# Spare rows for each skipped round of the expert tiles, integer row numbers by VectorE, and the last addition of x on Pool

## What is computed

```python
probs = softmax(flat @ gate_W)                    # flat: 2048 rows, 8 experts
topk_w, topk_idx = top_k(probs, 2); combine = one_hot(topk_idx) weighted, summed to 1
out = 0.5 * gelu(flat @ shared_W + shared_b)
for e in range(8):
    h = gelu(flat @ W1[e] + b1[e])
    out = out + combine[:, e:e + 1] * (h @ W2[e] + b2[e])
out = (out - mean) * rsqrt(var + eps) * gamma + beta
x = x + out
```

## Time and profile before

| What | us |
|---|---|
| Median of three timed runs | 948.01 |
| Lowest, highest | 945.2, 948.39 |
| The profiled execution: its own time | 945.59 |
| Its span, first to last instruction | 943.8 |

### The profile page before, as it was taken

The page is one execution under the profiler, slowest core; times in us unless marked ns, Lnnn a source line. Parts: engine busy times, 40 slices in busy tenths (PEclk is TensorE's granted clock), DMA queues, the critical chain, the costliest instruction groups (busy, mean ns, idle before and its releaser), DMA issues.

```text
span 943.8 us, 13190 instructions
## 1 busy us (share of the span) xinstructions
PE 797.0 (84%) x4073; PEld 392.5 (42%) x4074; DVE 389.8 (41%) x1042; ACT 413.8 (44%) x517; POOL 168.6 (18%) x161
## 2 busy tenths in 40 slices
PE   2876899999999999896979974289999999999820
PEld 1333223233222222232434443157666766666510
DVE  4793410111143343463445544264444444444227
ACT  2345488887898988633323321211111111111103
POOL 2030100100000000101004404772222222222330
PEclk9988799999999999987989987599999999999975
DMA  5759929874315320070021136454444444444334
GB/s 126 177 160 198 276 42 267 152 215 54 48 22 68 43 25 0 0 279 0 1 91 46 46 123 234 152 192 114 118 115 113 112 112 113 111 114 117 64 81 119
DMA packets 77288, 104.79 MB, mean 111 GB/s; under 512 B 9164, under 2 KB 62374, under 8 KB 77092
## 3 DMA queue, kind: packets, MB, share of 16 engines
q1 hardware_dynamic: 69948, 92.75, 38.4%
q0 software_dynamic: 7296, 11.47, 6.3%
HBM read 66.04 MB, written 38.16 MB: 110 GB/s over the span
## 4 chain that ended last, share of the span: by engine, by line
PE 66%; DVE 12%; DMA 7%; ACT 6%; issue 5%; SPq 2%; POOL 1%; ACTq 0%; POOLq 0%; DVEq 0%
PE ps L1833 12%; PE ps L1850 12%; PE ps L1548 9%; PE ps L1526 9%; PE ps L1642 6%; ACT arena L721 4%; PE ps L1841 3%; DMA sums_by_row<-arena 3%; PE ps L1714 2%; PE ps L1686 2%; PE ps L1654 1%; PE ps L1643 1%; DVE arena L889 1%; PE ps L1562 1%; DMA q_parts<-arena 1%
## 5 line engine op out<-in xcount | busy, mean ns | idle before, releaser
L721 ACT ACTIVATE arena<-ps 128x1024 f32<-128x1024 f32 x256 | 247.8, 1021 | 50.0 <-PE ps L1548 48.5
L1548 PE MATMUL ps<-arena 99*128 99x512 bf16 x512 | 143.6, 389 | 10.2 <-ACT arena L721 3.2
L1526 PE MATMUL ps<-arena 128*32 128x512 f32 x1024 | 137.0, 608 | 0.0
L1850 PE MATMUL ps<-arena,xh_tag 128*128 x560 | 128.2, 382 | 8.8 <-DVE xh_tag L1299 8.3
L1833 PE MATMUL ps<-arena 128*128 x280 | 129.6, 607 | 0.6 <-ACT arena L800 0.6
L1850 PEld LDWEIGHTS ps<-arena,xh_tag 128*128 128x128 f32 x560 | 104.7, 192 | 22.8 <-issue 9.7
L800 ACT COPY arena<-ps 128x256 f32<-128x256 f32 x35 | 13.0, 372 | 201.4 <-PE ps L1823 201.4
L644 POOL DMA_INDIRECT sums_by_row<-arena x39 | 61.3, 1572 | 213.0 <-DVE arena L1321 197.8
L1548 PEld LDWEIGHTS ps<-arena 99*128 99x128 bf16 x512 | 36.2, 98 | 115.5 <-ACT arena L721 96.6
L1294 DVE TENSOR_TENSOR xh_tag<-ps,xh_tag 128x1024 f32<-128x1024 f32 x35 | 42.9, 1224 | 89.7 <-PE ps L1833 89.6
L1833 PEld LDWEIGHTS ps<-arena 128*128 128x128 f32 x280 | 51.7, 195 | 53.5 <-issue 53.4
(11 more groups left out here) (228 smaller groups left out, 836.9 us busy)
## 6 DMA issues: line engine op xcount, KB each, us to landing
xh_tag<-in_L_ffn_b SPq DMA_DIRECT2D x35, 512.0 KB, 3.8
rows_by_expert<-arena SPq DMA_DIRECT2D x9, 1950.0 KB, 19.1
arena<-in_L_ffn_W SPq DMA_DIRECT2D x16, 1024.0 KB, 10.9
arena<-k_parts SPq DMA_DIRECT2D x48, 128.0 KB
arena<-q_parts SPq DMA_DIRECT2D x48, 128.0 KB
arena<-rows_by_expert SPq DMA_DIRECT2D x35, 130.0 KB, 2.1
arena<-in_L_ffn_b SPq DMA_DIRECT2D x35, 128.0 KB, 3.1
q_parts<-arena SPq DMA_DIRECT2D x8, 384.0 KB, 4.0
```

Source lines behind the costliest of these rows:

```text
L721: nc.scalar.activation(probs[:, st % 2, h, :], ps[:, 2 * (u % 2):2 * (u % 2) + 2, :].rearrange("p a n -> p (a n)"), ACT.Exp, scale=float(D ...
L1526: last = nc.tensor.matmul(ps[32 * h:32 * h + 32, 4 + half, :], v_grp[buf][:, kt, h, :], probs[:, kt % 2, h, 512 * half:512 * (half + 1)], ...
L1548: last = nc.tensor.matmul(ps[:, 2 * (u % 2) + half, :], k_stk[buf][:, h, P * st:P * (st + 1)], q_stk[buf][:, h, 512 * half:512 * (half + 1 ...
L1850: last = nc.tensor.matmul(ps[:, 6, 0:D], hid_t[:, k, :], w2_sb[:, bass.ds(e, 1), k, :].squeeze(1), start=(k == 0), stop=(k == HID // P - 1))
```

## The change

- `sums_dram` gets six more blocks of 128 spare rows, one for each result of a pair that may be skipped; the zero fill L442 covers seven blocks instead of one.
- Pool writes, once, spare row numbers for these six results into `row_if_run` (one iota). A pair that runs overwrites its two columns with the true row numbers (VectorE, from `row_at`); a skipped pair leaves the spare ones.
- Pool's additions 32 to 37 no longer wait for one another. They count in a semaphore of their own, `cond_set`; inside a pair that runs, VectorE waits before a result until the addition before has landed. Pool and VectorE wait once for all six before results 38 and 39.
- VectorE's tag copy writes the row numbers as integers. Pool's instructions for them go. Instead of `row_at_set`, `tags` waits until the addition that read the buffer has landed.
- At the end VectorE only multiplies by gamma; Pool waits for `x_final` and adds to x.

```diff
--- before.py
+++ after.py
...
-        sums_dram = nc.dram_tensor("sums_by_row", [(NT + 1) * P, D], F32).ap()
+        sums_dram = nc.dram_tensor("sums_by_row", [(NT + 1 + 2 * (PAIRS - SURE)) * P, D], F32).ap()
...
-        row_f, row_weight = (r.take([P, 2]) for _ in range(2))
+        row_weight = r.take([P, 2])
         row_at = r.take([P, 2], U32)
-        spare_f, row_over = (r.take([P, 1]) for _ in range(2))
+        row_if_run = r.take([P, 2 * (PAIRS - SURE)], U32)
...
-            sp.dma_start(sums_dram[NT * P:, :], zeros).then_inc(sums_zero, 16)
+            n = 1 + 2 * (PAIRS - SURE)
+            sp.dma_start(sums_dram[NT * P:, :].rearrange("(t p) f -> p t f", p=P),
+                         zeros.unsqueeze(1).to_broadcast([P, n, D])).then_inc(sums_zero, 16)
...
-            sp.wait_ge(sums_set, 16 * (SLOT_TILES + 1))
+            sp.wait_ge(sums_set, 16 * (2 * SURE + 4))
...
-            nc.gpsimd.iota(spare_f, [[0, 1]], base=NT * P, channel_multiplier=1,
-                           allow_small_or_imprecise_dtypes=True).then_inc(spare_set, 1)
+            nc.gpsimd.iota(row_if_run, [[P, 2 * (PAIRS - SURE)]], base=(NT + 1) * P, channel_multiplier=1).then_inc(spare_set, 1)
             nc.gpsimd.tensor_tensor(x_sb[:, :, :], x_sb[:, :, :], ffn_b_sb.unsqueeze(1).to_broadcast([P, NT, D]),
                                     ALU.add).then_inc(x_shifted, 1)
             pool.wait_ge(sums_zero, 16)
-            pool.wait_ge(spare_set, 1)
-
-            def rows_of(buf, n):
-                pool.wait_ge(tag_ready, n)
-                nc.gpsimd.tensor_copy(row_at[:, buf:buf + 1], row_f[:, buf:buf + 1]).then_inc(row_at_set, 1)
-
-            def rows_if_run(buf, n, i):
-                pool.wait_ge(tag_ready, n)
-                nc.gpsimd.tensor_tensor(row_over, row_f[:, buf:buf + 1], spare_f, ALU.subtract).then_inc(spare_set, 1)
-                pool.wait_ge(spare_set, n - 2 * SURE)
-                nc.gpsimd.tensor_scalar(row_at[:, buf:buf + 1], row_over, run_f[:, i - SURE:i - SURE + 1], spare_f[:, 0:1],
-                                        ALU.mult, ALU.add).then_inc(row_at_set, 1)
-
-            def add_result(buf, n):
+
+            def add_result(buf, n, rows, landed):
                 pool.wait_ge(y_ready, n)
-                pool.wait_ge(row_at_set, n)
+                nc.gpsimd.indirect_dma_start(
+                    out=sums_dram, out_offset=bass.IndirectOffsetOnAxis(ap=rows, axis=0),
+                    in_=y_sb[:, buf, :], in_offset=None, compute_op=ALU.add).then_inc(landed, 16)
+
+            for n in range(1, 2 * SURE + 2):
                 pool.wait_ge(sums_set, 16 * n)
-                nc.gpsimd.indirect_dma_start(
-                    out=sums_dram, out_offset=bass.IndirectOffsetOnAxis(ap=row_at[:, buf:buf + 1], axis=0),
-                    in_=y_sb[:, buf, :], in_offset=None, compute_op=ALU.add).then_inc(sums_set, 16)
-
-            rows_of(0, 1)
-            add_result(0, 1)
-            for n in range(2, 2 * SURE + 2):
-                rows_of((n - 1) % 2, n)
-                add_result((n - 1) % 2, n)
-            for i in range(SURE, PAIRS):
-                for o in range(2):
-                    rows_if_run(1 - o, 2 * i + (o + 2), i)
-                    add_result(1 - o, 2 * i + (o + 2))
-            for n in range(SLOT_TILES - 1, SLOT_TILES + 1):
-                rows_of((n - 1) % 2, n)
-                add_result((n - 1) % 2, n)
+                add_result((n - 1) % 2, n, row_at[:, (n - 1) % 2:(n - 1) % 2 + 1], sums_set)
+            for n in range(2 * SURE + 2, 2 * PAIRS + 2):
+                c = n - 2 * SURE - 2
+                add_result((n - 1) % 2, n, row_if_run[:, c:c + 1], cond_set)
+            pool.wait_ge(cond_set, 16 * 2 * (PAIRS - SURE))
+            for n in range(2):
+                pool.wait_ge(sums_set, 16 * (2 * SURE + 2 + n))
+                add_result(1 - n, SLOT_TILES - 1 + n, row_at[:, 1 - n:2 - n], sums_set)
+
+            pool.wait_ge(x_shifted, 2 + B)
+            for n, (first, end) in enumerate(ROUNDS):
+                rows = slice(first, end)
+                pool.wait_ge(x_final, n + 1)
+                nc.gpsimd.tensor_tensor(x_sb[:, rows, :], x_sb[:, rows, :], y_in[:, rows, :], ALU.add).then_inc(out_ready, 1)
...
-            def tags(buf, n, tile, rows_read=None):
+            def tags(buf, n, tile, rows_read=None, taken=None):
                 if rows_read is not None:
-                    dve.wait_ge(row_at_set, rows_read)
+                    dve.wait_ge(sums_set, 16 * taken + 16)
                     dve.wait_ge(y_ready, rows_read)
-                nc.vector.tensor_copy(row_f[:, buf:buf + 1], xs_in[:, buf, D:D + 1])
+                nc.vector.tensor_copy(row_at[:, buf:buf + 1], xs_in[:, buf, D:D + 1])
                 nc.vector.scalar_tensor_tensor(out=row_weight[:, buf:buf + 1], in0=xs_in[:, buf, D + 1:D + 2],
                                                scalar=expert_rank[:, tile], in1=xs_in[:, buf, D + 2:D + 3],
                                                op0=ALU.is_equal, op1=ALU.mult).then_inc(tag_half, 1)
             tags(1, 2, bass.ds(1, 1))
             result(0, 1, 16)

-            def round_dve(i, first=False):
+            def round_dve(i, first=False, may_be_skipped=False):
                 for o in range(2):

                     turned_hidden(2 * i + (o + 2))
                     sum_hidden(o, 2 * i + (o + 3), 16 * i + 32)
-                    tags(o, 2 * i + (o + 3), bass.ds(2 * i + (o + 2), 1), 2 * i + (o + 1))
-                    result(1 - o, 2 * i + (o + 2), 16 * i + 16 * (o + 1), None if first and o == 0 else 32 * i + 16 * (o + 1))
+                    tags(o, 2 * i + (o + 3), bass.ds(2 * i + (o + 2), 1), 2 * i + (o + 1),
+                         min(2 * i + (o + 1), 2 * SURE + 1) if may_be_skipped else 2 * i + (o + 1))
+                    if may_be_skipped:
+                        n = 2 * i + (o + 2)
+                        dve.wait_ge(tag_ready, n)
+                        if n == 2 * SURE + 2:
+                            dve.wait_ge(spare_set, 1)
+                        nc.vector.tensor_copy(row_if_run[:, n - 2 * SURE - 2:n - 2 * SURE - 1], row_at[:, 1 - o:2 - o]).then_inc(row_copied, 1)
+                        dve.wait_ge(row_copied, n - 2 * SURE - 1)
+                        if n == 2 * SURE + 2:
+                            dve.wait_ge(sums_set, 16 * n)
+                        else:
+                            dve.wait_ge(cond_set, 16 * (n - 2 * SURE - 2))
+                    result(1 - o, 2 * i + (o + 2), 16 * i + 16 * (o + 1),
+                           None if first and o == 0 or may_be_skipped else 32 * i + 16 * (o + 1))

             round_dve(0, True)
             with dve.Fori(1, SURE) as i:
                 round_dve(i)
             for i in range(SURE, PAIRS):
-                may_run(nc.vector, dve, i, round_dve, lambda i: (
+                may_run(nc.vector, dve, i, lambda i: round_dve(i, may_be_skipped=True), lambda i: (
+                    (row_copied, 2 * (i - SURE), 2),
                     (h_sum, 2 * i + 2, 2), (ht_ready, 2 * i + 1, 2), (y_ready, 2 * i + 1, 2),
                     (tag_half, 2 * i + 2, 2), (tag_ready, 2 * i + 2, 2), (y_sum, 2 * i + 1, 2)))
             final = nc.vector.value_load(last_tile[0:1, 0:1], min_val=2 * SURE + 2, max_val=SLOT_TILES - 1)
             turned_hidden(SLOT_TILES - 1)
             sum_hidden(0, SLOT_TILES, 16 * (PAIRS + 2))
-            tags(0, SLOT_TILES, bass.ds(final, 1), SLOT_TILES - 2)
-            result(1, SLOT_TILES - 1, 16 * (PAIRS + 1), 16 * (SLOT_TILES - 2))
+            tags(0, SLOT_TILES, bass.ds(final, 1), SLOT_TILES - 2, 2 * SURE + 1)
+            dve.wait_ge(cond_set, 16 * 2 * (PAIRS - SURE))
+            result(1, SLOT_TILES - 1, 16 * (PAIRS + 1))
             turned_hidden(SLOT_TILES)
-            result(0, SLOT_TILES, 16 * (PAIRS + 2), 16 * (SLOT_TILES - 1))
-            dve.wait_ge(x_shifted, 2 + B)
+            result(0, SLOT_TILES, 16 * (PAIRS + 2))

             def finish(n):

                 rows = slice(*ROUNDS[n])
                 dve.wait_ge(out_normed, n + 1)
                 tiles = ROUNDS[n][1] - ROUNDS[n][0]
-                link(nc.vector.tensor_tensor(y_in[:, rows, :], y_in[:, rows, :], ffn_g_sb.unsqueeze(1).to_broadcast([P, tiles, D]), ALU.mult))
-                nc.vector.tensor_tensor(x_sb[:, rows, :], x_sb[:, rows, :], y_in[:, rows, :], ALU.add).then_inc(out_ready, 1)
+                nc.vector.tensor_tensor(y_in[:, rows, :], y_in[:, rows, :], ffn_g_sb.unsqueeze(1).to_broadcast([P, tiles, D]), ALU.mult)\
+                    .then_inc(x_final, 1)

```

More of the change, by code:

```diff
@@ L301, in decoder_layer @@
             "xs_ps", "xs_ready", "h_ps", "h_sum", "h_act", "ht_ps", "ht_ready", "y_ps", "y_ready"))
-        tag_half, tag_ready, row_at_set, y_sum, spare_set = (sem(n) for n in (
-            "tag_half", "tag_ready", "row_at_set", "y_sum", "spare_set"))
```

(3 more changed lines are left out.)

## The result

The changed kernel took 939.08 us in the median of four runs (936.42 to 939.45) against 947.09 us for the kernel before; the ratio is 0.9911, with a 95% interval of 0.9884 to 0.9938. It is faster by 8.0 us, within the forecast range (932.7 to 943.5) and 2.3 us above the forecast. Its profiled execution took 938.73 us with a span of 936.9; the span before was 943.8. The lines of the file have moved: L644 is now L632, L1374 is L1380, L1359 is L1365, L1377 is L1383, L1319 is L1311, and Pool's addition to x is L651.

A forecast was written before the change was run, and what follows sets the result against it. TensorE's pace bounds the expert tiles, then seven additions waiting on each other bound the end. Removing those waits (9.5 us) and moving x's last additions to Pool (0.5) gives 10.0 off 946.8: 936.8 us, range 932.7 to 943.5.

The forecast's parts named there:

- What bounds the kernel: Expert tiles run at TensorE's pace, 7.98 us each; after the last real tile, a chain of waiting additions bounds the end.
- the string of additions: After the last tile run, seven additions into sums_by_row, each waiting for the one before, from 883.07 to 914.63 us.
- part 4: Kernel's tail: moving the last additions to x from VectorE to Pool was to gain 0.5 us.
- Pace of back-to-back additions: Skipped rounds: additions 34 to 37 issue 1.87 us apart (possibly 1.28), the last at 890.55, landing at 894.30.
- The rival of a serial queue: Skipped rounds: the queue finishes each addition before the next, gain only 0.1 + 0.5 us, 946.2 us; chance 0.08.
- the half-serial variant: Skipped additions serial only behind their descriptors: last lands at 896.0, costs 1.8 us, total 938.6; counted within the forecast's 0.84.
- Addition 39: Last addition into the sums: issues 1.09 us after its result's instruction starts, at 901.35, landing at 905.1 against 914.63.
- Part 2: Expert tiles: VectorE writes the row numbers instead of Pool and waits for landings; cost 0, up to 0.3 us once.
- Part 3: Larger zero fill, 896 KB instead of 128, on SP's queue: cost 0, upper bound 1 us, even at seven times 5.84.
- The lock in part 4: Tail: Pool's additions block some VectorE instructions; period 3.47 us instead of 4.05, gain 0.5 us, 2.8 without exclusion.
- part 1: Skipped rounds without waits between their additions: gain 9.5 us, 8.0 with the clock lowered, 9.7 with no loss.
- The base: Whole kernel's starting time: 946.8 us, the mean of the profiled execution and three timed runs, from which gains are subtracted.

The follow-up runs named there:

- part 4 alone: The kernel before with only the six last additions to x moved from VectorE to Pool, all else as before: ratio 1.0016.

## Why the prediction held, and what it missed

- *What bounds the kernel* and *the string of additions*: right. Putting the waits back took the whole gain away (1.0035), with part 4's loss of 1.9 us left in.
- *Pace of back-to-back additions*: 1.87 us forecast, 1.84 measured; the last issued at 890.36 (forecast 890.55). Result 38 started at 894.31 (894.33), TensorE's last product at 896.51 (896.6), in 3.72 us at a granted clock of 1.00. The scatters' gap of 0.30 in the earlier trace rows was the right row to borrow from. The rival of a serial queue is excluded, the half-serial variant too: the last addition had landed at 894.1, where that variant had 896.0.
- *Addition 39*: forecast 1.09 us behind the start of L1311, measured 1.56. I looked at the work that Pool loses and not at the order of its waits, which the diff shows. Gain of the stretch 8.9 us instead of 9.5. The experiment with the other order gives the 0.5 back.
- *Part 2 is free*: right. VectorE waited for a landing three times, 4.1 us in all, 3.1 of it for the first, slow one; TensorE stayed busy for the 208 us from 651 to 859 in both kernels, and additions 33 differ by 0.1 us. From the first scatter of sorted rows to addition 33 pass 386.2 to 387.8 us in the twelve profiles of this study, whichever engine makes the row numbers. Pool's issue came 0.5 us later in each steady tile (1.56 us behind the start of L1311 instead of 1.09), and that was covered too.
- *Part 3 is free*: right. The larger fill held SP for 5.84 us, no longer than the small one in the earlier trace rows, and the next issue is at 208.9. The bound of seven times 5.84 was far off: the 5.84 us did not grow with the bytes, only the landing did (14.7 us after the start instead of 12.5). That SP stood there for the transfers ahead is my reading; no run tests it.
- *The lock in part 4*: right in its places and nearly in its sizes. The period came out at 3.42 (3.47 forecast), Pool's additions at 1.80 and 1.26 (1.81 and 1.27), and the tail at a gain of 0.8 us (0.5). The Trainium skill (SBUF — State Buffer, Who interferes with whom) gives the two kinds of instruction that are held, and the runs agree with both: with Pool's addition one column long, L1380 is back at 0.17 us and the last multiplication, with two operands in SBUF, at 0.69.
- *Where it failed*: in part 4 the end of the span moved with the last addition to x (now at 940.29, forecast 939.75, gain 0.5), as if what follows it took the same 3.5 us whoever does the addition. It is 6.2 us if Pool does that addition, since Pool's DRAIN ends about 6 us after Pool's last instruction. So part 4 is worth 0.8 - 2.7 = -1.9 us instead of +0.5. The trace before did show that DRAIN, 7.7 us long, but fully hidden; moving the end of Pool's last instruction from 912.44 to 930.69 took its cover away. The prediction never named the work that hides it. The range held all the same, because part 1 carries the sum and part 4, wrong in sign, is small beside it.
- *The base.* The forecast stood on 946.8 and the median before became 947.09. Against the profiled execution the forecast was 935.6 and the changed one took 938.73, 3.1 us more: 2.4 of it is part 4 and 0.6 the issue of addition 39. The gain by medians, 8.0 us, is between the 6.9 us of the two spans and the forecast 10.0; that it came nearer to the forecast than the spans did is luck. The clock of the last product explains little of it. That product took 5.10 us in the profile before, at a granted clock of 0.72, and 6.67 to 6.76 us at 0.54 to 0.55, close to the lower level (1.2 GHz), in the three other profiles with the old waits (part 4 alone, and the two with a memset on Pool). But from the issue of addition 33 to the first load of the sums these three took 31.7 to 32.0 us against 31.6, since in the profile before addition 39 stood waiting for the landing of addition 38 while its result was done (909.24, issue at 910.88). So the lower clock of those three costs at most 0.2 to 0.4 us of the whole; the rest of the 1.1 us is not resolved, and the time at which addition 33 issues alone differs by 2.8 us between executions (881.0 to 883.8).

## What to carry to other kernels

Look at which waits in a chain guard work that is skipped, and give that work places of its own, so that it needs no order; here the stretch with these waits became 8.9 us shorter, more than the 6.9 us by which the span shrank. Before an engine gets the last work of a program, look in the closing instructions how long its DRAIN takes and what it is hidden under; here Pool's help gained 2.0 us where its DRAIN ended before the last store and lost 1.9 where it didn't. Where Pool works beside VectorE, list VectorE's instructions by operands: two in SBUF, or a tensor_scalar in SBUF however short, stand for what is left of Pool's instruction; BATCH_NORM with its one operand did not (1.07 us beside Pool's addition as without it).

## What the runs showed of the hardware

- Pool's DRAIN at the end of the program ended 5.9 to 6.0 us after Pool's last instruction ended in every profile of this study, whatever that instruction was: an indirect DMA (912.44 to 918.4, before), an addition of 512 or 768 columns (930.69 to 936.7; 926.39 to 932.3), an addition of one column (924.44 to 930.4), a memset of one column (940.15 to 946.1). VectorE's ended 0.04 us after its last instruction (940.29 to 940.33, before).
- A VectorE tensor_scalar over two or three columns is held for the rest of Pool's addition: 0.93 and 0.53 us instead of 0.17, odd and even counts alike.
- Four accumulating indirect DMAs on one queue went 1.84 us apart; they landed 3.7 to 5.3 us after their start, the last at 894.1, before result 38 began (894.31). TensorE's two products beside them took 5.39 and 3.62 us, as in the kernel before.
- Of two waits ahead of a Pool DMA, it costs 0.5 us if the one on the separate instruction is fulfilled last (1.56 against 1.09 us behind the start of L1311). In the changed kernel that is the wait for y_ready, L631, recorded 33 times as a semaphore instruction of its own.
- TensorE's last product took 3.72 us at a granted clock of 1.00 after 1.42 us of idle time, and 5.10 to 6.76 us at 0.72 to 0.54 after 8.0 to 10.0 us of it; the longest idle time (10.0) did not give the longest product (5.72, at 0.64). The clock figures are means over the product, in parts of 2.4 GHz.
